# The order of a group's rows in device memory: channel by channel, or with the rows of channels eight apart next to each other

## The chip, the cores and the metric

The kernel runs on one core of a Trainium2 chip. Time is the device time of one execution in microseconds (us); it is 320.35 us as the median of 3 runs before the change (320.22 to 320.51).

## The reference, cut to what matters

```python
def _L0_cond_ref(x, subjects, weights):        # x: (128, 128, 1024), weights: (8, 128, 128), all f32
    w = weights[subjects]                      # one of 8 matrices for each of the 128 samples
    out = jnp.einsum('bct,bcd->bdt', x, w)
    return out
x = x + _L0_cond_ref(x, itok_B_0_7, L0_cond_weights)
```

Every sample is a matrix of 128 channels by 1024 times. It is multiplied by the weight matrix of its subject, and the sample itself is added. 64 MiB come in and 64 MiB go out.

## The kernel before, in words

The host lays x out by groups of GROUP = 4 samples: in a group each of the 128 channels has one row that holds its 4 samples of 1024 floats one behind the other, 16 KiB in all. A group is a block of 2 MiB, with the rows in the order of the channels (line 149). The output has the same layout and is turned back on the host (lines 157 and 158). There are 32 groups.

On the chip a ring of SLOTS = 8 slots in SBUF holds 8 groups, with the channels on the 128 partitions. The work of one group goes through these steps.

- SyncE (SP) issues the loads: first the weights (line 63), then the first 8 groups (line 65) with no wait, then the other 24 (lines 69 and 70), each once the store of the group that held the slot has landed.
- VectorE (DVE) adds the unit matrix to all 8 weight matrices once (line 111), so that one matmul gives product and residual together.
- GpSimd (POOL) reads the subject of each sample (line 84), waits at each group's first sample for its load (line 87) and copies the chosen matrix to one of 4 buffers (line 91).
- TensorE (PE) multiplies, two matmuls of 512 columns a sample (line 102), into one of 4 PSUM buffers of 1024 columns.
- DVE writes the products of even samples back into the slot (line 117), ScalarE (ACT) those of odd ones (line 128). The result takes the place of its own input.
- ACT issues the store of the group behind its last sample (line 133), after it has waited for both drains.

A load and a store each move one 2 MiB block. Loads go to the queue of SP (q1 in the profile), stores to that of ACT (q10); both are worked off by the same 16 DMA engines. `x_loaded[s]` and `stored[s]` are semaphores by slot; each takes 16 from every finished DMA. Line 137 is the end of the kernel: it waits for the last store of each slot.

Of the kernel before, what the change touches and what calls it, by code (L numbers as in the profile page):

```python
# [11 lines left out]
GROUP = 4  # L12

BUFS = 4
BANK = 512
DMA = 16


def subject_mix_kernel(nc: bass.Bass, x: bass.AP, subjects: bass.AP, weights: bass.AP, out: bass.AP):

    groups, channels, row = x.shape
    times = row // GROUP
    samples = groups * GROUP
    turns = groups // SLOTS
    per_turn = SLOTS * GROUP
    banks = times // BANK

    _, n_subjects, mixed = weights.shape
    assert channels == mixed == weights.shape[0] == 128 and banks * BANK == times and turns * SLOTS == groups
    assert GROUP == BUFS and 2 * BUFS == banks * BUFS  # L30

    with ExitStack() as ctx:
        def sem(name):
            return ctx.enter_context(nc.semaphore(name))


        ring = ctx.enter_context(nc.sbuf_tensor("ring", [channels, SLOTS, GROUP, times], F32))
        loaded = ctx.enter_context(nc.sbuf_tensor("loaded", [channels, n_subjects, mixed], F32))
        table = ctx.enter_context(nc.sbuf_tensor("table", [channels, n_subjects, mixed], F32))
        ones = ctx.enter_context(nc.sbuf_tensor("ones", [channels, mixed], F32))  # L40
        unit = ctx.enter_context(nc.sbuf_tensor("unit", [channels, mixed], F32))
        selected = ctx.enter_context(nc.sbuf_tensor("selected", [channels, BUFS, mixed], F32))
        subject_row = ctx.enter_context(nc.sbuf_tensor("subject_row", [1, samples], I32))
        products = ctx.enter_context(nc.psum_tensor("products", [mixed, BUFS, times], F32))

        subjects_loaded = sem("subjects_loaded")
        weights_loaded = sem("weights_loaded")
        ones_ready = sem("ones_ready")
        unit_ready = sem("unit_ready")
        table_ready = sem("table_ready")  # L50
        x_loaded = [sem(f"x_loaded{s}") for s in range(SLOTS)]
        stored = [sem(f"stored{s}") for s in range(SLOTS)]

        weights_selected = [sem(f"weights_selected{j}") for j in range(per_turn)]

        product_ready = sem("product_ready")
        even_drained = sem("even_drained")
        odd_drained = sem("odd_drained")

        with nc.Block() as block:  # L60
            @block.sync
            def _(sp):
                sp.dma_start(loaded[:], weights[:]).then_inc(weights_loaded, DMA)  # L63
                for s in range(SLOTS):
                    sp.dma_start(ring[:, s].rearrange("p j t -> p (j t)"), x[s]).then_inc(x_loaded[s], DMA)  # L65
                for group in range(SLOTS, groups):
                    turn, s = divmod(group, SLOTS)

                    sp.wait_ge(stored[s], turn * DMA)
                    sp.dma_start(ring[:, s].rearrange("p j t -> p (j t)"), x[group]).then_inc(x_loaded[s], DMA)  # L70

            @block.gpsimd
            def _(pool):
                nc.gpsimd.memset(ones[:], 1.0).then_inc(ones_ready, 1)  # L74
                pool.wait_ge(ones_ready, 1)

                nc.gpsimd.affine_select(unit[:], ones[:], [[-1, mixed]], ALU.is_equal, 0.0,  # L77
                                        base=0, channel_multiplier=1).then_inc(unit_ready, 1)
                pool.wait_ge(subjects_loaded, DMA)
                pool.wait_ge(table_ready, 1)  # L80
                for i in range(samples):
                    turn, j = divmod(i, per_turn)

                    subject = pool.value_load(subject_row[0:1, i:i + 1]).with_bounds(min_val=0, max_val=n_subjects - 1)  # L84
                    if j % GROUP == 0:

                        pool.wait_ge(x_loaded[j // GROUP], turn * DMA + DMA)
                    if i >= BUFS:

                        pool.wait_ge((even_drained, odd_drained)[i % 2], (i - BUFS) // 2 + 1)  # L90
                    nc.gpsimd.tensor_copy(selected[:, i % BUFS:i % BUFS + 1, :],  # L91
                                          table[:, bass.ds(subject, 1), :]).then_inc(weights_selected[j], 1)

            @block.tensor
            def _(pe):
                with pe.Fori(0, turns) as turn:
                    for j in range(per_turn):
                        s, g = divmod(j, GROUP)

                        pe.wait_ge(weights_selected[j], turn + 1)  # L100
                        for n in range(banks):
                            last = nc.tensor.matmul(products[:, j % BUFS, n * BANK:(n + 1) * BANK],  # L102
                                                    selected[:, j % BUFS, :],
                                                    ring[:, s, g, n * BANK:(n + 1) * BANK], start=True, stop=True)
                        last.then_inc(product_ready, 1)

            @block.vector
            def _(dve):
                dve.wait_ge(unit_ready, 1)
                dve.wait_ge(weights_loaded, DMA)  # L110
                nc.vector.tensor_tensor(table[:], loaded[:],  # L111
                                        unit[:].unsqueeze(1).to_broadcast([channels, n_subjects, mixed]),
                                        ALU.add).then_inc(table_ready, 1)
                for i in range(0, samples, 2):

                    dve.wait_ge(product_ready, i + 1)
                    nc.vector.tensor_copy(ring[:, i // GROUP % SLOTS, i % GROUP, :],  # L117
                                          products[:, i % BUFS, :]).then_inc(even_drained, 1)

            @block.scalar  # L120
            def _(act):
                act.dma_start(subject_row[:], subjects.rearrange("(a b) -> a b", a=1)).then_inc(subjects_loaded, DMA)
                for i in range(1, samples, 2):
                    group = i // GROUP
                    s = group % SLOTS

                    act.wait_ge(product_ready, i + 1)
                    nc.scalar.copy(ring[:, s, i % GROUP, :], products[:, i % BUFS, :]).then_inc(odd_drained, 1)  # L128
                    if i % GROUP == GROUP - 1:

                        act.wait_ge(even_drained, (i + 1) // 2)
                        act.wait_ge(odd_drained, (i + 1) // 2)  # L132
                        act.dma_start(out[group], ring[:, s].rearrange("p j t -> p (j t)")).then_inc(stored[s], DMA)


        for s in range(SLOTS):
            nc.scalar.wait_ge(stored[s], turns * DMA)
# [21 lines left out]
```

## Time and profile before

| | |
|---|---|
| median of 3 runs | 320.35 us (320.22 to 320.51) |
| the profiled execution | 320.11 us |
| its span, first to last instruction | 318.7 us |
| moved by DMA in the span | 134.80 MB, 423 GB/s on average |
| mean granted clock of TensorE | 0.942 |
| PE, DVE, ACT, POOL busy | 76%, 25%, 21%, 12% of the span |

The page of the profile gives shares of the span by engine, a row of 40 slices of the span (8 us each) with the share of time in which the DMA engines were busy and what they moved, the DMA queues with packets and bytes, the chain of waits that ended last, and groups of instructions. A packet is one row of 16 KiB for x and the output. Semaphore increments are packets of a few bytes of their own. A view by stretches gives the same for chosen parts of the span; its DMA share can read a little over 1, since a packet is counted whole in the stretch in which it starts. The view of DMA issues gives the time in which an issue holds its queue's engine, and the time from issue to landing.

### The profile page before, as it was taken

The page shows a single profiled execution, that of the slowest core. Times are in us where ns is not written, and L with a number is a line of the kernel's source. Part 1 is how long each engine was busy: PE and PEld are TensorE (multiplying, and loading weights), DVE is VectorE, ACT ScalarE, POOL GpSimd, SP SyncE. Part 2 cuts the span into 40 slices and gives each one's busy share as a digit, 9 for nine tenths or more (in the row PEclk, how much of TensorE's full clock was granted, in tenths as well). Part 3 has the DMA queues.
Part 4 walks back from the last instruction along what each step waited for, and adds up shares of the span by engine and source line. Part 5 has one row for each costly group of instructions (what it writes and reads, how often), then busy time and mean ns, then how long its engine had stood idle before and what let it go on. Part 6 is the DMA issues. An engine that isn't in the chain of part 4 may idle for free.

```text
span 318.7 us, 1718 instructions
## 1 busy us (share of the span) xinstructions
PE 242.5 (76%) x512; PEld 101.0 (32%) x512; DVE 79.6 (25%) x65; ACT 66.1 (21%) x65; POOL 38.6 (12%) x134
## 2 busy tenths in 40 slices
PE   0799999787868886669868668768698686787840
PEld 0344444233323332223333223323233232233310
DVE  1133433331313321223313133212233131331310
ACT  1033223211222212121212222112212122211220
POOL 0111111011110011100111101111001111011100
PEclk9999999997998999998979999979989799997995
DMA  8999999999999999999999999999999999999996
GB/s 300 430 424 393 428 429 426 432 434 436 436 428 430 428 428 430 431 432 437 436 428 430 428 428 430 432 431 434 431 434 430 430 428 430 430 434 434 430 436 290
DMA packets 9368, 134.80 MB, mean 423 GB/s; under 512 B 1041, under 2 KB 1042, under 8 KB 1170
## 3 DMA queue, kind: packets, MB, share of 16 engines
q1 hardware_dynamic: 4752, 67.64, 50.1%
q10 hardware_dynamic: 4610, 67.11, 49.2%
q14 instruction: 5, 0.04, 0.0%
q8 instruction: 1, 0.02, 0.0%
HBM read 67.63 MB, written 67.11 MB: 423 GB/s over the span
## 4 chain that ended last, share of the span: by engine, by line
DMA 81%; PE 10%; another core or an unknown queue 2%; ACT 1%; SPq 1%; POOLq 1%; issue 0%; DVE 0%; ACTq 0%
DMA ring<-x 51%; DMA out<-ring 30%; PE products L102 10%; ACT ring L128 1%; SPq L65 1%; POOLq L84 0%; DVE ring L117 0%; SPq L63 0%; POOLq L91 0%; ACTq L132 0%; POOLq L90 0%
## 5 line engine op out<-in xcount | busy, mean ns | idle before, releaser
L102 PE MATMUL products<-ring,selected 128*128 128x512 f32 x512 | 242.5, 631 | 63.6 <-POOL selected L91 63.6
L102 PEld LDWEIGHTS products<-ring,selected 128*128 128x128 f32 x512 | 101.0, 202 | 204.2 <-issue 119.1
L117 DVE COPY ring<-products 128x1024 f32<-128x1024 f32 x64 | 78.4, 1225 | 221.2 <-PE products L102 221.2
L128 ACT COPY ring<-products 128x1024 f32<-128x1024 f32 x64 | 64.8, 1012 | 239.7 <-PE products L102 239.7
L91 POOL COPY selected<-table 128x128 f32 x128 | 37.9, 296 | 261.7 <-DMA ring<-x 206.2
L111 DVE TENSOR_TENSOR table<-loaded,unit 128x1024 f32<-128x1024 f32 x1 | 1.2, 1226 | 4.7 <-DMA loaded<-weights 4.7
L128 ACT ACT_TABLE_LOAD x1 | 1.3, 1283 | 1.4 <-PEq L145 1.4
L77 POOL TENSOR_SCALAR_AFFINE_SELECT unit<-ones 128x128 f32<-128x128 f32 x1 | 0.3, 294 | 0.1
L74 POOL MEMSET ones<- 128x128 f32 x1 | 0.2, 205 | 0.3 <-POOLq L145 0.3
L145 POOL MEMSET const-float32-0.0<- 128x1 f32 x1 | 0.1, 99 | 0.3 <-issue 0.3
L145 POOL MEMSET const-bfloat16-1.0<- 128x1 bf16 x1 | 0.1, 102 | 0.0
L145 POOL MEMSET const-uint8-127<- 128x1 uint8 x1 | 0.1, 102 | 0.0
L145 POOL MEMSET const-float32-1.0<- 128x1 f32 x1 | 0.1, 99 | 0.0
## 6 DMA issues: line engine op xcount, KB each, us to landing
ring<-x SPq DMA_DIRECT2D x32, 2048.0 KB, 37.1
out<-ring ACTq DMA_DIRECT2D x32, 2048.0 KB, 30.8
loaded<-weights SPq DMA_DIRECT2D x1, 512.0 KB, 3.8
subject_row<-subjects ACTq DMA_DIRECT2D x1, 0.5 KB
```

Of the source, the lines that this page charges most:

```text
L65: sp.dma_start(ring[:, s].rearrange("p j t -> p (j t)"), x[s]).then_inc(x_loaded[s], DMA)
L74: nc.gpsimd.memset(ones[:], 1.0).then_inc(ones_ready, 1)
L77: nc.gpsimd.affine_select(unit[:], ones[:], [[-1, mixed]], ALU.is_equal, 0.0, base=0, channel_multiplier=1).then_inc(unit_ready, 1)
L91: nc.gpsimd.tensor_copy(selected[:, i % BUFS:i % BUFS + 1, :], table[:, bass.ds(subject, 1), :]).then_inc(weights_selected[j], 1)
L102: last = nc.tensor.matmul(products[:, j % BUFS, n * BANK:(n + 1) * BANK], selected[:, j % BUFS, :], ring[:, s, g, n * BANK:(n + 1) * BANK] ...
L111: nc.vector.tensor_tensor(table[:], loaded[:], unit[:].unsqueeze(1).to_broadcast([channels, n_subjects, mixed]), ALU.add).then_inc(table_r ...
L117: nc.vector.tensor_copy(ring[:, i // GROUP % SLOTS, i % GROUP, :], products[:, i % BUFS, :]).then_inc(even_drained, 1)
L128: nc.scalar.copy(ring[:, s, i % GROUP, :], products[:, i % BUFS, :]).then_inc(odd_drained, 1)
L145: nc = bacc.Bacc("TRN2", target_bir_lowering=False, num_devices=1)
```

## The change

The host splits the 128 channels as 16 parts of EACH = 8 (channel = 8 u + i, with u from 0 to 15 and i from 0 to 7) and writes the rows of a group in the order i, u: first channels 0, 8, 16, ... 120, then 1, 9, ... 121, and so on. In the block of 2 MiB the rows of channels 8 u + i and 8 (u + 1) + i are neighbours, 16 KiB apart; those of two channels in sequence are 16 rows (256 KiB) apart. The DRAM side of every load and store is an access pattern of three dimensions, 16 (u) by 8 (i) by 4096 floats, in the order of the channels; the SBUF side stays 128 partitions by 4096 floats. So each channel ends in the same partition as before, and nothing on the chip but the addresses of loads and stores differs.

```diff
+EACH = 8
...
-    groups, channels, row = x.shape
+    groups, each, parts, row = x.shape
+    channels = each * parts
...
+    x_rows = [x[group].rearrange("i u f -> u i f") for group in range(groups)]
+    out_rows = [out[group].rearrange("i u f -> u i f") for group in range(groups)]
...
-                    sp.dma_start(ring[:, s].rearrange("p j t -> p (j t)"), x[s]).then_inc(x_loaded[s], DMA)
+                    sp.dma_start(ring[:, s].rearrange("p j t -> p (j t)"), x_rows[s]).then_inc(x_loaded[s], DMA)
...
-                    sp.dma_start(ring[:, s].rearrange("p j t -> p (j t)"), x[group]).then_inc(x_loaded[s], DMA)
+                    sp.dma_start(ring[:, s].rearrange("p j t -> p (j t)"), x_rows[group]).then_inc(x_loaded[s], DMA)
...
-                        act.dma_start(out[group], ring[:, s].rearrange("p j t -> p (j t)")).then_inc(stored[s], DMA)
+                        act.dma_start(out_rows[group], ring[:, s].rearrange("p j t -> p (j t)")).then_inc(stored[s], DMA)
...
-    laid = x.reshape(groups, GROUP, channels, times).transpose(0, 2, 1, 3).reshape(groups, channels, GROUP * times)
+    parts = channels // EACH
+    laid = x.reshape(groups, GROUP, parts, EACH, times).transpose(0, 3, 2, 1, 4)
+    laid = laid.reshape(groups, EACH, parts, GROUP * times)
...
-    mixed = result.results[0]["out"].reshape(groups, channels, GROUP, times)
-    return np.ascontiguousarray(mixed.transpose(0, 2, 1, 3).reshape(samples, channels, times))
+    mixed = result.results[0]["out"].reshape(groups, EACH, parts, GROUP, times)
+    return np.ascontiguousarray(mixed.transpose(0, 3, 2, 1, 4).reshape(samples, channels, times))
```

## Rows read from the trace of the kernel before

**Rows 1.** The page: the chain of waits that ended last, shares by engine and line.
```profile
DMA 81%; PE 10%; another core or an unknown queue 2%; ACT 1%; SPq 1%; POOLq 1%; issue 0%; DVE 0%; ACTq 0%
DMA ring<-x 51%; DMA out<-ring 30%; PE products L102 10%; ACT ring L128 1%; SPq L65 1%; POOLq L84 0%; DVE ring L117 0%; SPq L63 0%; POOLq L91 0%; ACTq L132 0%; POOLq L90 0%
```

**Rows 2.** The page: the DMA lines of the 40 slices, and its queues.
```profile
DMA  8999999999999999999999999999999999999996
GB/s 300 430 424 393 428 429 426 432 434 436 436 428 430 428 428 430 431 432 437 436 428 430 428 428 430 432 431 434 431 434 430 430 428 430 430 434 434 430 436 290
...
q1 hardware_dynamic: 4752, 67.64, 50.1%
q10 hardware_dynamic: 4610, 67.11, 49.2%
```

**Rows 3.** The view of DMA queues, stretch 120:200: packets, MB, share of 16 engines.
```profile
q10 hardware_dynamic: 1182, 17.24, 50.3%
q1 hardware_dynamic: 1188, 17.22, 50.3%
```

**Rows 4.** By stretches: start:end us, length, PE, PEld, DVE, ACT, POOL, PEclk, DMA share, GB/s.
```profile
0.00:2.00 2.00, 0.00 (x0) 0.00 (x0) 0.00 (x0) 0.64 (x1) 0.70 (x6) 1.00 0.26 29
2.00:4.00 2.00, 0.00 (x0) 0.00 (x0) 0.00 (x0) 0.64 (x1) 0.00 (x0) 1.00 0.92 303
4.00:6.00 2.00, 0.00 (x0) 0.00 (x0) 1.23 (x1) 0.00 (x0) 0.00 (x0) 1.00 0.98 406
6.00:8.00 2.00, 0.00 (x0) 0.00 (x0) 0.00 (x0) 0.00 (x0) 0.00 (x0) 1.00 1.08 459
12.00:16.00 4.00, 4.00 (x7) 1.67 (x6) 1.23 (x1) 0.00 (x0) 0.30 (x1) 1.00 1.00 430
22.00:28.00 6.00, 6.00 (x16) 2.65 (x15) 2.16 (x2) 2.02 (x2) 0.89 (x3) 1.00 1.00 369
120.00:200.00 80.00, 60.24 (x129) 24.85 (x128) 19.60 (x16) 17.21 (x17) 9.48 (x32) 0.96 1.01 431
312.00:316.00 4.00, 0.00 (x0) 0.00 (x0) 0.00 (x0) 0.00 (x0) 0.00 (x0) 0.50 0.97 414
316.00:318.70 2.70, 0.00 (x0) 0.00 (x0) 0.00 (x0) 0.00 (x0) 0.00 (x0) 0.50 0.12 49
```

**Rows 5.** Who waited for whom, whole span: us in total, times, longest us.
```profile
POOL selected L91 <- DMA ring<-x: 206.2, 28, 8.3
PE products L102 <- POOL selected L91: 63.6, 27, 10.0
```

**Rows 6.** The same for SP's queue: us in total, times, longest us.
```profile
SPq L70 <- DMA out<-ring: 247.3, 24, 31.1
```

**Rows 7.** The issues by line: ns min/median/max, first and last start.
```profile
L65 SPq DMA_DIRECT2D ring<-x x8: 424/436/643, 1.2 to 4.8; - x8
L70 SPq DMA_DIRECT2D ring<-x x24: 327/328/328, 36.4 to 260.5; - x24
L133 ACTq DMA_DIRECT2D out<-ring x32: 338/338/376, 21.1 to 307.2; - x32
```

**Rows 8.** Landing: the page's issues (KB each, us), then stores alone (min/median/max).
```profile
ring<-x SPq DMA_DIRECT2D x32, 2048.0 KB, 37.1
loaded<-weights SPq DMA_DIRECT2D x1, 512.0 KB, 3.8
DMA to landing us min/median/max: 11.5/30.8/32.5
```

**Rows 9.** The DMA queues in 22:28, around the first store: packets, MB, share.
```profile
q1 hardware_dynamic: 119, 1.69, 80.0%
q10 hardware_dynamic: 32, 0.52, 20.4%
```

## Prediction

> **What bounds the kernel now.** I read the chain of waits first: 81% of the span is DMA, 51% loads and 30% stores, and only 10% TensorE [rows 1]. A chain can run through transfers that wait for their turn, so next come the slices: the 16 DMA engines are nine tenths busy or more in 38 of 40, and move 424 to 437 GB/s in all of these but one, with loads and stores at 50.1% and 49.2% of the engines' time [rows 2]. Those two are 99.3% of 318.7 us, or 316.5 us of work for each engine. The kernel is bound by DMA engine time, not by latency and not by an order of work.
>
> The waits agree: GpSimd stands 206.2 us for loads in total and TensorE only 63.6 us for GpSimd, while SP stands 247.3 us for stores before it may load again [rows 5, 6]. Compute has time to spare, and a slot is refilled as soon as its store has landed.
>
> How good is the engine time itself? In 120:200 the stores take 50.3% of 16 x 80 us for 17.24 MB. That is 643.8 us for 1052 rows of 16384 bytes: 612 ns a row, or 26.8 GB/s an engine. The loads give the same, 50.3% for 17.22 MB, 613 ns [rows 3]. Reading from device memory and writing to it cost the same to within 0.2%, in a mixed stream. Where only loads run (12:16, 430 GB/s) and where both do (120:200, 431) the rate is one and the same [rows 4]. If the order of rows in memory cost anything in the steady state, I would expect it to differ by direction or by mix. I read 612 ns as what one engine needs for 16 KiB, whatever lies at the memory's side.
>
> **The sum of the span.** 134.80 MB at 431 GB/s are 312.8 us. To these come the stretches that move less, each by length x (1 - rate / 431) [rows 4]: 0:2 at 29 GB/s 1.87 us, 2:4 at 303 0.59, 4:6 at 406 0.12, 6:8 at 459 -0.13, 22:28 at 369 0.86, 312:316 at 414 about 0.16, 316:318.7 at 49 2.39. Together 5.9 us, and 318.7 in all, the span. The profiled execution took 320.11 us, so 1.4 us lie outside of the span, and it is 0.24 us below the median of 320.35. My numbers are the span's changes added to the median.
>
> **The change part by part.**
>
> *The steady term, 312.8 us.* Bytes, rows (8192 of 16 KiB), queues and engines stay. Only addresses move. Below, the term has no room: no slice of 8 us is over 437 GB/s, and 437 in place of 431 would be 1.4%, 4.3 us, a bound that the chip would have to hold for all of the span where it touches it in five slices (four of 436, one of 437), which differ from the mean by three rows of 16 KiB in some 210, counted in one slice or the next [rows 2]. Above, the one row in which something at the memory's side goes slower is 22:28, 369 GB/s [rows 4]; if all ran so, the term would be 365 us. I take the value of the long stretch, 431, since both directions hold it: 0 us. The ends stay for the range.
>
> *The stall at 22:28, 0.86 us.* The first store is issued at 21.1 [rows 7]. In 22:28 the sixteen engines have 16 x 6 = 96 us. The loads hold 80.0% of it for 1.69 MB, which is 103 rows: 96 us x 0.800 / 103 = 746 ns a row, against 613 in the steady state. The stores beside them take 96 x 0.204 / 32 = 612 ns [rows 3, 9]. So 103 load rows are slowed by 133 ns on average when writing begins, 13.7 us over 16 engines, the same 0.86. This is the only place in the trace where rows are slow. It is tied to the first write to the output, which is still there after the change, so I leave it as it is; between nothing left (-0.86 us) and twice as long (+0.86 us).
>
> *Issue of the DMAs.* The pattern at the memory's side has one dimension more. The issues hold their engine 328 ns (loads), 338 (stores) and 436 (the first eight) [rows 7]. If an issue grew to the longest seen, 643 ns, it would be 0.3 us more on each of 24 loads and 32 stores. What hides it: a load is 37.1 us from issue to landing [rows 8], in which half of 431 GB/s moves 8.0 MB, so nearly four loads of 2.1 MB are in the queue at a time and the engines never run out; for the last store, 11.5 us to landing at 431 GB/s are 5.0 MB, of which 2.9 MB are stores ahead of it. Without that cover it would be 24 x 0.3 = 7 us, at most, for loads. At the start there is less cover: the first x rows come behind the weights, whose issue stays as it is and whose rows land 3.8 us after it [rows 8]. I take 0, and 0.2 us as the upper end for the first issue. A cheaper issue would gain nothing, by the same cover.
>
> *Compute and order.* POOL, PE, DVE and ACT get the same bytes in the same partitions. A load that lands 0.3 us later would be met by a GpSimd that waits 206.2 us for loads anyway [rows 5]: what is late is only the group's store, and a store joins a queue 30.8 us deep [rows 8]. Nothing new waits.
>
> Sum: 0 us. A change of 0.64 us (0.2%) is about what a measurement of this kernel can tell from none.
>
> **A rule that speaks against it.** The rows show that in the layout of before, where the rows of one group are one run of 2 MiB, each takes 612 ns and no more [rows 3]. The Trainium skill, "DMA: Bandwidth & Descriptors", Latency and other measured facts, has copies between memory tensors slow down as the pitch between partitions' rows becomes a large power of two: 207 GB/s a direction at 512 KiB where a full rate is 214, and 103 at 4 MiB. By an estimate from that page a 3.3% lower rate would put some 10 us on the time; after the change channels in sequence are 256 KiB apart and those eight apart 16 KiB, so the rule reads either way, and no trace here shows a pitch that slows.
>
> **The rivals.**
>
> *R1, the stall at the first store goes.* If it comes from sixteen writes (and sixteen reads) that open sixteen distant places, neighbours may pass it quicker. For it: it is the only place with slow rows. Against it: the loads alone began at distant places too and run at 430 in 12:16 [rows 4]. Gain at most 0.86 us, 319.5 us. 0.13.
>
> *R2, neighbouring rows collide.* Sixteen engines that start one step together would now read one stretch of 256 KiB instead of sixteen places 128 KiB apart; if the memory spreads its load by addresses coarser than a row, they would sit on fewer parts of it. Place: every load and store, in the first of the eight steps above all, since engines drift apart later. Price: if one step in eight runs at the 369 GB/s of 22:28 [rows 4], the steady term grows by 1/8 x (431/369 - 1) = 2.1%, 6.6 us, giving 326.9 us. It decides once the mean row is over 613.3 ns (612 + 0.2%). For it: the memory's side did slow rows once. Against: that a row needs no more than 612 ns leaves unknown how much room the memory has, and it is the weakest argument on both sides. 0.17.
>
> *R3, the sides are split differently.* The memory's side counts 16 x 8, the SBUF side 128. The generator of packets may hand the rows to engines in another way, and two engines may then go to the same part of SBUF at one time. The trace of before has no row for it. It would cost between nothing and a doubling of the steady term (two engines sharing what one has now); by the nearest row, 369 GB/s throughout, it is 365 - 313 = 52 us, 372 us. 0.10. The Trainium skill, "SBUF — State Buffer", Door 1: The DMA port swizzle, lets partitions p and p + 32 share a port, and "DMA: Bandwidth & Descriptors", The descriptor swizzle, gives each engine just the partitions of one port, in a transfer of 128 partitions; by those pages a split into eight partitions in sequence would make engines share ports, and no run here shows it.
>
> *R4, the change doesn't do what it says.* If an engine's eight rows are not eight channels in sequence, the sixteen rows of one step are not the sixteen neighbours. Then the addresses are only shuffled in the block, and the time stays at 320.3 us. By the Trainium skill, "DMA: Bandwidth & Descriptors", The descriptor swizzle (engine e of the first eight takes partitions 4e to 4e+3 and 32 more), neighbouring engines would start at channels 4 apart, 1 MiB apart in the new layout; no run here shows which rows an engine takes. 0.15, with the same number as my forecast.
>
> **How the numbers follow.** The forecast, that nothing is changed since the row time is the engines' own, has 0.45; with R4 that is 0.60 for within 0.2%. R1 gives 0.13 for faster; R2 and R3 0.27 for slower. Predicted: 320.3 us. Its own range is 319.8 to 320.9. The range of 8 in 10 takes in R1 (319.3, with 0.2 for the runs) and most of R2 (to 327.5), and leaves out R3 and the far part of R2, some 0.15.
>
> **What would show it.** Right: 612 ns a row in both queues in 120:200; 428 to 437 GB/s in the slices; the same 4752 and 4610 packets; the dip at 22:28 still there; issues of 330 to 650 ns and SP still waiting over 240 us. Wrong: a row time over 613.3 ns or a steady rate below 430 (R2; R3 if it is below 400 or the packets differ in number), a rate of 425 or more in 22:28 (R1), or idle DMA engines in the middle, which would mean that the issue had lost its cover. The step that I trust least is that 612 ns is the engine's own time and that the memory has room behind it.

## The result and the profile after

The changed kernel takes 374.83 us (median of 5 runs, 371.8 to 387.34), the kernel before 320.35 beside it (5 runs, 320.0 to 321.46): a ratio of 1.167, 95% interval 1.165 to 1.170. It was forecast at 320.3 with a range up to 327.5. The ratio leaves out the slowest execution, 387.34 us, which is the one profiled below (its granted clock is 0.879, that of the other four 0.878 to 0.892), so the sums that follow stand to 387 and not to 375.

The slices and the queues of the page, beside [rows 2]:

```profile
DMA  8999999999999999999999999999999999999968
GB/s 200 216 211 295 341 343 405 397 408 385 384 377 370 350 355 370 353 366 363 363 370 375 385 379 382 374 368 357 360 359 363 363 362 375 406 408 401 350 192 190
...
q1 hardware_dynamic: 4752, 67.64, 52.3%
q10 hardware_dynamic: 4610, 67.11, 46.5%
```

The same packets, the same bytes, engines as busy as before, and 5% to 56% less moved in a slice: each packet takes longer. The view by stretches of the changed kernel, beside [rows 4] (loads alone run in the first two), and its DMA queues in 120:200, beside [rows 3] (packets, MB, share of 16 engines):

```profile
4.00:20.00 16.00, 4.53 (x6) 2.04 (x7) 1.94 (x2) 0.00 (x0) 1.17 (x4) 1.00 1.02 218
12.00:16.00 4.00, 0.53 (x1) 0.50 (x2) 0.00 (x0) 0.00 (x0) 0.58 (x3) 1.00 1.04 221
22.00:28.00 6.00, 5.32 (x14) 2.10 (x13) 1.90 (x2) 1.26 (x2) 1.17 (x4) 1.00 1.02 216
120.00:200.00 80.00, 53.66 (x104) 21.90 (x103) 15.93 (x14) 13.16 (x13) 8.21 (x28) 0.88 1.01 363
```

```profile
q1 hardware_dynamic: 998, 14.52, 52.8%
q10 hardware_dynamic: 997, 14.52, 48.0%
```

In 120:200 the sixteen engines have 16 x 80 = 1280 us, and 14.52 MB are 886 rows: a load row takes 0.528 x 1280 / 886 us = 763 ns and a store row 0.480 x 1280 / 886 us = 693 ns, where both took 612 to 613. Where only loads run (12:16) the rate is 221 GB/s in place of 430. That is very nearly half, and a first hint of the cause: two engines doing the work of one. Against 431 GB/s, and by slices of 9.65 us, the first three slices lose 14.9 us, the last two 10.7 and the 35 between the rest of the 73.1 us by which the span is over 312.8: 47.5 us. Before, the whole loss was 5.9.

The issues of the changed kernel (lines 72 and 77 are the old 65 and 70), beside [rows 7], and who waited, beside [rows 5, 6]:

```profile
L72 SPq DMA_DIRECT2D ring<-x x8: 581/598/617, 1.2 to 5.7; - x8
L77 SPq DMA_DIRECT2D ring<-x x24: 536/537/537, 46.0 to 308.6; - x24
```

```profile
POOL selected L98 <- DMA ring<-x: 309.7, 32, 13.8
```

```profile
SPq L77 <- DMA out<-ring: 289.5, 24, 39.7
```

An issue holds SP 537 ns in place of 328. It delays nothing that shows, as SP waits 289.5 us for stores and the DMA engines are nine tenths busy or more from the second slice to the 38th. Compute waits more because loads come later; it is not the cause.

### The profile page after: what moved, and what is told of

Read it like the earlier page. It is cut to its first block, busy times and chain, and to the rows that moved or that the text cites. A ratio compares the mean times of both kernels' runs of the same rounds, so it can differ in the third digit from the quotient of the medians.

```text
span 385.9 us, 1718 instructions
## 1 busy us (share of the span) xinstructions
PE 266.6 (69%) x512; PEld 108.8 (28%) x512; DVE 79.6 (21%) x65; ACT 66.1 (17%) x65; POOL 38.2 (10%) x134
## 2 busy tenths in 40 slices
DMA packets 9368, 134.80 MB, mean 349 GB/s; under 512 B 1041, under 2 KB 1042, under 8 KB 1170
## 3 DMA queue, kind: packets, MB, share of 16 engines
q1 hardware_dynamic: 4752, 67.64, 52.3%
q10 hardware_dynamic: 4610, 67.11, 46.5%
## 4 chain that ended last, share of the span: by engine, by line
another core or an unknown queue 48%; PE 23%; DMA 11%; DVE 9%; POOLq 3%; issue 2%; SPq 1%; ACT 0%; POOL 0%
PE products L109 23%; DMA ring<-x 11%; DVE ring L124 9%; POOLq L91 2%; SPq L72 0%; POOLq L98 0%; ACT ring L135 0%; POOL selected L98 0%; POOLq L97 0%; SPq L70 0%
## 5 line engine op out<-in xcount | busy, mean ns | idle before, releaser
L109 PE MATMUL products<-ring,selected 128*128 128x512 f32 x512 | 266.6, 680 | 106.8 <-POOL selected L98 106.8
L109 PEld LDWEIGHTS products<-ring,selected 128*128 128x128 f32 x512 | 108.8, 218 | 263.7 <-POOL selected L98 132.5
```

## The experiments

Two accounts were set against each other, and within the first stands a question of its own. **S**, rival R3: the pattern of 16 x 8 makes each engine take the eight channels of one outer step, partitions 8u to 8u + 7, and two engines then use one way into SBUF. A way is meant as the part of the path to SBUF that certain partitions have in common; two engines whose partitions lie on one way are called partners, and they are in step when they use it at the same time. **M**, rival R2: rows that are neighbours in memory collide. The question is whether engines lose only while they are in step.

### The pattern without the new order, and the order without the pattern

The order of rows of before, with an unused row behind each eight, so that the pattern must stay 16 x 8 (against the changed kernel, cut; x and out are of groups, 16, 9, row):

```diff
-    x_rows = [x[group].rearrange("i u f -> u i f") for group in range(groups)]
-    out_rows = [out[group].rearrange("i u f -> u i f") for group in range(groups)]
+    x_rows = [x[group, :, 0:each, :] for group in range(groups)]
+    out_rows = [out[group, :, 0:each, :] for group in range(groups)]
...
```

> Theory S (split): the 16 x 8 pattern at the memory's side makes each engine take eight channels in sequence, and two engines then meet at one part of SBUF. Theory M (memory): neighbouring rows, 16 KiB apart, collide in device memory. This kernel has the order of rows of before, but with one unused row behind every eight, so that the pattern is 16 x 8 and can't be written as 128 rows. S expects the time of the changed kernel, 365 to 390 us, with loads alone (4:20) at about 218 GB/s and 1.2 us a row. M expects 320 to 322 us and 426 to 430 GB/s there.

Measured: 372.86 and 380.64 us, and 1.21 us a row with loads alone. By stretches, nearly the rates of the changed kernel (218, 216 and 363 GB/s):

```profile
4.00:20.00 16.00, 4.39 (x7) 1.91 (x8) 1.90 (x2) 0.00 (x0) 1.18 (x4) 1.00 1.02 219
22.00:28.00 6.00, 5.14 (x13) 2.03 (x12) 1.91 (x2) 1.07 (x2) 1.19 (x4) 1.00 1.00 218
120.00:200.00 80.00, 57.75 (x110) 23.59 (x110) 15.93 (x14) 14.17 (x14) 8.29 (x28) 0.87 1.01 367
```

The rows lie in the old order, and the loss is all there. So the new order in memory is not needed for it. The opposite test keeps the pattern of 128 rows and puts the rows 512 KiB apart (against the kernel before; the other loads and the stores alike):

```diff
-                    sp.dma_start(ring[:, s].rearrange("p j t -> p (j t)"), x[s]).then_inc(x_loaded[s], DMA)
+                    sp.dma_start(ring[:, s].rearrange("p j t -> p (j t)"), x[:, s]).then_inc(x_loaded[s], DMA)   # x: (channels, groups, row)
```

> The pattern of 128 rows of before, but each channel's rows of all groups lie one behind the other, so that the rows of one transfer are 512 KiB apart. S expects 320 to 322 us, since the split stays. M, in its general form (where a step's rows lie in memory sets the rate), expects a time clearly off 320: 325 to 335 us at this pitch, or more.

Measured: 320.6 us, ratio 1.0022 (1.0003 to 1.004), so at most 0.4% is lost, and in 120:200 the rate is the old one:

```profile
120.00:200.00 80.00, 63.15 (x131) 25.72 (x129) 20.35 (x17) 17.16 (x17) 9.39 (x32) 0.94 1.01 431
```

### Neighbours with another pattern: EACH = 4 and EACH = 2

```diff
-EACH = 8
+EACH = 4
```

> The changed kernel with EACH = 4: rows of channels four apart are neighbours, the pattern is 32 x 4. M expects 365 us or more, since the rows of channels in one step are neighbours as before or more so. S expects 365 to 390 us if engines still take eight channels in sequence, and about 320 us if a count of 32 lets the generator hand out blocks of four as it does with 128; either way it says nothing against S, but 320 us falls M.

Measured: 320.3 us, ratio 1.0008 (0.9996 to 1.002). Stretches, and the issues:

```profile
4.00:20.00 16.00, 10.22 (x21) 4.61 (x22) 3.68 (x3) 2.03 (x2) 2.37 (x8) 1.00 1.01 429
22.00:28.00 6.00, 6.00 (x15) 2.66 (x14) 2.25 (x2) 1.85 (x2) 0.89 (x3) 1.00 1.03 374
120.00:200.00 80.00, 61.57 (x131) 25.08 (x129) 20.31 (x17) 16.90 (x17) 9.48 (x32) 0.96 1.01 430
```

```profile
L77 SPq DMA_DIRECT2D ring<-x x24: 534/534/535, 35.1 to 260.7; - x24
```

Rows that are neighbours in memory are again those of a fixed distance in channels, and nothing is lost. M falls. So does any account by the third dimension of the pattern or the longer issue: this kernel has both, 534 ns an issue, at no cost. That part of the prediction's sum (0 us for the issue) is measured here by itself.

> The changed kernel with EACH = 2, a pattern of 64 x 2. With 32 x 4 the time was that of before. If the generator needs outer counts that make blocks of four channels or less, 64 x 2 is as good: 320 to 321 us. If it splits along the outer count into sixteen runs in sequence unless the count is one that it knows, 64 x 2 may fall back to eight channels in sequence: 365 to 390 us. S allows both; M (neighbouring rows in memory) is out already.

With EACH = 2 the time was 320.1 us, ratio 0.9997 (0.9986 to 1.0008). So 64 x 2, 32 x 4 and 128 rows are equal, and 16 x 8 stands alone.

### A direct test of the ways into SBUF

The order and the one-count pattern of before, but each transfer cut in two, of partitions 0 to 63 and 64 to 127 (the stores alike; the waits count two DMAs):

```diff
-                    sp.dma_start(ring[:, s].rearrange("p j t -> p (j t)"), x[s]).then_inc(x_loaded[s], DMA)
+                    sp.dma_start(ring[0:64, s].rearrange("p j t -> p (j t)"), x[s, 0:64]).then_inc(x_loaded[s], DMA)
+                    sp.dma_start(ring[64:128, s].rearrange("p j t -> p (j t)"), x[s, 64:128]).then_inc(x_loaded[s], DMA)
```

> The order of rows of before and patterns of one count (64 rows), but each load and store is cut into two DMAs, of channels 0 to 63 and 64 to 127. M expects 320 to 323 us. S in its port form (partitions 0 to 63 reach half of SBUF's ports) expects loads alone at about half the rate, 215 to 220 GB/s, and a time of 360 us or more; if the engines do not share by halves of the partitions, 320 to 323 us.

Measured: 388.13 and 400.95 us. The first stretch:

```profile
4.00:20.00 16.00, 4.52 (x6) 1.94 (x7) 1.93 (x2) 0.00 (x0) 1.17 (x4) 1.00 1.02 215
```

Half the rate again, with neither the new order in memory nor the 16 x 8 pattern. What the cut changes is the size of a transfer and which partitions the sixteen engines write at one time; to tell these two apart, the next kernel cuts at 32 and 96 instead, three DMAs a group:

```diff
+                    sp.dma_start(ring[32:96, s].rearrange("p j t -> p (j t)"), x[s, 32:96]).then_inc(x_loaded[s], DMA)
+                    sp.dma_start(ring[0:32, s].rearrange("p j t -> p (j t)"), x[s, 0:32]).then_inc(x_loaded[s], DMA)
+                    sp.dma_start(ring[96:128, s].rearrange("p j t -> p (j t)"), x[s, 96:128]).then_inc(x_loaded[s], DMA)
```

> The order of rows of before; each transfer is cut into three, of channels 32 to 95, 0 to 31 and 96 to 127. S with the map in which partitions 32 apart share a way into SBUF: the 64 of the first reach all the ways, four channels to an engine, at full rate; the 32 of each other reach half of them. Loads alone then average 431 / (1/2 + 1/2 x 2) = 287 GB/s, if the engines stay in step, more if the two small ones overlap; 215 to 220 would mean that any transfer under 128 partitions is slow, 425 to 430 that the cut at 64 was special. Time: 330 to 360 us by S.

Measured: 365.0 us (363.44 and 366.58), and for loads alone

```profile
4.00:20.00 16.00, 7.04 (x12) 3.16 (x13) 2.45 (x2) 1.01 (x1) 1.18 (x4) 1.00 1.01 275
```

275 GB/s against 287 worked out, and well over the 215 of the cut at 64, though the transfers are smaller and more. The time came out 5 us over the range given for it. Stretches of 1 us show the two rates by turns, here those in the middle of the start:

```profile
12.00:13.00 1.00, 0.04 (x1) 0.04 (x1) 0.00 (x0) 0.00 (x0) 0.29 (x1) 1.00 1.08 459
13.00:14.00 1.00, 1.00 (x2) 0.48 (x3) 0.00 (x0) 0.00 (x0) 0.65 (x3) 1.00 0.98 360
14.00:15.00 1.00, 1.00 (x3) 0.48 (x2) 0.00 (x0) 0.00 (x0) 0.24 (x1) 1.00 1.14 246
15.00:16.00 1.00, 1.00 (x3) 0.48 (x2) 0.00 (x0) 0.00 (x0) 0.00 (x0) 1.00 1.01 213
```

The packet records of the trace say the same: of the 269 load rows that start in 4:20, 98 take under 640 ns and 100 over 1150. In the changed kernel none of 213 takes under 1000 ns. So the 64 partitions of the middle are written at the full rate, and a transfer of 64 partitions is not slow for being small; 0 to 63 together, or 64 to 127 together, are slow. The Trainium skill, "SBUF — State Buffer", Door 1: The DMA port swizzle, has partitions 32 apart share one of sixteen ports, 0 to 63 reaching eight of them. These two runs agree with that map: 215 GB/s is half of the 429 before, and 275 is 4% under the 287.

### Loads alone, stores alone

Only x, or only the output, in the changed layout and pattern. The first, against the changed kernel (the second does the same to x_rows instead):

```diff
-    out_rows = [out[group].rearrange("i u f -> u i f") for group in range(groups)]
+    out_rows = [out[group] for group in range(groups)]
```

> Only the loads use the 16 x 8 pattern; the output keeps the order and the 128-row pattern of before. Theory S (engines that take eight channels in sequence meet at one part of SBUF): loads alone (4:20) at about 218 GB/s as in the changed kernel, the stores alone at the end at 425 to 438 GB/s, and a time between the two kernels, 335 to 360 us. Rival S2 (the slow part is the packets' own generation or decoding, whatever the direction): the same for the start, but in the mixed part the stores' rows keep 612 ns.

> Only the stores use the 16 x 8 pattern. S: loads alone (4:20) at 426 to 430 GB/s, stores alone at the end at about 190 to 230 GB/s as in the changed kernel, 335 to 360 us in all. If the loss were one of loads alone (writes into SBUF), the time would be 320 to 322 us.

Measured: 362.9 us with the loads (ratio 1.133, 1.128 to 1.138), 330.95 and 348.57 us with the stores. The queues in 120:200, first the kernel with changed loads:

```profile
q1 hardware_dynamic: 1096, 16.09, 52.7%
q10 hardware_dynamic: 1083, 15.79, 48.4%
```

and the one with changed stores:

```profile
q10 hardware_dynamic: 1172, 17.11, 51.2%
q1 hardware_dynamic: 1168, 16.97, 49.6%
```

With changed loads a load row takes 687 ns and a store row 643, though the stores are as before; they share their engines with slow loads, which may be why. Loads alone run at 216 GB/s there. With changed stores a store row takes 628 ns and a load row 613. In these executions, then, writing SBUF costs more than reading it; but the second is the one of 330.95 us, and its other execution took 348.57, so this is not shown in general. S2, by which the stores would keep 612 ns, does not hold. The two losses, 42.6 and 10.7 to 28.3 us, add up to 53 to 71 where both changes together cost 54.5. The time with loads is 3 us over the range given.

Both ends missed their numbers. With changed loads the stores alone at the end (345:360) come to 268 GB/s in place of 425 to 438, but because the engines work for 63% of the time; a row takes 619 ns, as S has it. With changed stores the last four slices read 372, 318, 366 and 181 GB/s, above the 190 to 230 given in three of four. Here are the stores alone near the end, first of the changed kernel in 370:384, then of this one in 316:326:

```profile
q10 hardware_dynamic: 173, 2.57, 76.9%
```

```profile
q10 hardware_dynamic: 226, 3.21, 78.2%
```

The first are 0.769 x 16 x 14 / 157 us = 1.10 us a row, the second 0.782 x 16 x 10 / 196 us = 0.64 us. The same stores with the same pattern, alone in both, are near to doubled in one kernel and near to the old 612 ns in the other. So the pattern by itself doesn't set the size of the loss. How the engines stand to each other may; these lines don't show it.

The slices of the kernel with changed loads show the same for loads:

```profile
GB/s 205 215 217 308 367 391 414 402 398 387 393 396 393 409 407 391 395 386 400 385 404 409 337 405 420 427 416 414 409 403 398 400 398 362 351 375 387 404 248 266
```

The transfers run at 217 GB/s in the third slice, where they are alone; mixed with stores they run at 427 in the 26th and at 337 three slices before that. It is no fixed tax.

### How many engines: EACH = 16

The changed kernel with EACH = 16 in the place of 8.

> EACH = 16, a pattern of 8 x 16. If the outer counts set the number of engines (the largest number up to 16 that divides both 8 and 128), only 8 engines work, each on 16 channels in sequence, and engines 0 and 2, 1 and 3 and so on share a way when in step: about 107 GB/s with loads alone (a quarter of 431), at most 215 in the mixed part, 620 to 1000 us in all. If 16 engines stay, the packet share is near 100% and the time 320 to 390 us.

Measured: 682.6 us, ratio 2.131 (2.112 to 2.151). Stretches of this kernel:

```profile
4.00:20.00 16.00, 0.00 (x0) 0.00 (x0) 1.22 (x1) 0.00 (x0) 0.00 (x0) 1.00 0.50 108
120.00:200.00 80.00, 36.04 (x64) 14.75 (x64) 9.80 (x8) 8.10 (x8) 4.70 (x16) 0.75 0.51 211
```

```profile
q1 hardware_dynamic: 547, 8.44, 25.4%
q10 hardware_dynamic: 547, 8.44, 25.1%
```

The DMA share is 0.50: half of the engines work. The Trainium skill, "DMA: Bandwidth & Descriptors", Why a DMA increments its semaphore by 16 and not by 1, has a DMA use as many engines as the largest number up to 16 that divides both outer counts, which is eight here; the trace agrees with its 0.50. With loads alone they reach 108 GB/s, half of what eight engines can, or 1.22 us a row (0.500 x 16 x 16 us for 105 rows). In 120:200 they reach 211, and a row takes 631 (loads) and 624 ns (stores). The channels of an engine and their order are the same in both stretches, and the loss of half seen at the start is all but gone in the mix.

The numbers suggest why, by an estimate that no run tests. If a way passes two rows every 1.22 us, as loads alone show, then in the mix two partners, which each write one row in 631 + 624 = 1255 ns, ask for no more than it passes. That would fit an engine that is slow at writing by itself as well; this run doesn't exclude one. Nor does it tell why sixteen engines lose 16% in the mix and these eight 1.5%.

### Seven tries to move partners out of step

If engines meet only while in step, a lead of half a transfer (4 of an engine's 8 rows) should cure the start. Small extra transfers ahead of the groups were to give such leads, on 12, 8 or 4 engines; first into a spare tensor, then from memory to memory. The first of them:

```diff
+                sp.dma_start(spare[0:48, 0, :], x_rows[0][0:12, 0:4, :]).then_inc(shifted, DMA)
+                sp.dma_start(spare[0:16, 1, :], x_rows[0][0:4, 0:4, :]).then_inc(shifted, DMA)
```

> The changed kernel with two small extra loads into a spare tensor ahead of the groups: 4 rows each on engines 0 to 11 (outer count 12) and 4 more on engines 0 to 3 (outer count 4), so that engines 0-3, 4-7, 8-11, 12-15 stand 8, 4, 4 and 0 rows back. S-step: an engine with eight channels in sequence takes four of them through one way into SBUF and four through the next, and engines e and e+4 are on the same way when in step; four rows apart they never meet. Expected: loads alone (4:20) well above 218, up to 431 GB/s, and 325 to 355 us in all. Rival S-fixed: an engine whose channels lie on two ways is slow by itself, whatever its partner does: 218 GB/s and 370 us or more, plus 2.4 us for the extra rows.

> As the run before but 8 rows in place of 4 in each extra load: the partners stand 8 rows apart, a whole transfer, and so are in step again. S-step: loads alone at about 218 GB/s, 370 to 385 us. If a shift of any size helps (because it is only disorder that helps), the rate is as high as with 4 rows.

> Only engines 0 to 7 are put 4 rows back (one extra load with an outer count of 8). If partners are e and e+4, both stay in step: 218 GB/s in 4:20 and 368 to 385 us. If partners are e and e+8 (of two halves), all pairs are apart: up to 431 GB/s.

> Only engines 0 to 3 are put 4 rows back. Partners e and e+4: the pairs of the first eight engines are apart, those of the other eight in step, so loads alone run at (431 + 218) / 2 = 325 GB/s at the start, and the whole lies between the run with all pairs apart and the changed kernel, 345 to 372 us. S-fixed: 218 GB/s.

> As the first shifted kernel (4 rows on engines 0 to 11, 4 on 0 to 3), but the extra rows go to partitions 32 to 79 and 64 to 79 of the spare tensor. In the first one the extra loads themselves met: engines 8 to 11 wrote partitions 32 to 47, beside engines 0 to 3 on 0 to 15, so that the two groups came out of them by other than 4 rows. Counting each row at 611 ns, and at twice that where two engines are on one way (way = bits 2 to 4 and bit 6 of the partition), gives 260 GB/s for loads alone in 14:30 of the first and 390 to 396 here. S-step: 350 to 396 GB/s in 14:22. S-fixed, or a wrong map of the ways: no better than the first (266 to 299).

> The changed kernel with the same two extra transfers (4 rows on engines 0 to 11, 4 on 0 to 3), but from memory to memory, so that they touch no part of SBUF and can't meet there. S-step: engines e and e+4 then stand just 4 rows apart when the groups begin, and loads alone run at 400 to 431 GB/s in 14:22. If the way into SBUF pulls partners into step whatever their start, or if partners are others than e and e+4, the rate is 210 to 290 as in the runs with the spare tensor.

> The same with 8 rows in each extra transfer: partners stand a whole transfer apart and are in step. S-step: 210 to 225 GB/s in 22:30, where the extra rows are through, and 375 to 390 us in all. If a shift of any size helps, the rate is as high as with 4 rows.

| kernel | us (2 runs) | 4:20, GB/s | 14:22, GB/s | expected, GB/s |
|---|---|---|---|---|
| the change | 371.8 to 387.34 (5 runs) | 218 | 209 | |
| 4 rows, spare | 365.91, 372.34 | 222 | 276 | up to 431 (4:20) |
| 8 rows, spare | 383.14, 389.08 | 216 | 219 | 218 (4:20) |
| 4 rows on engines 0 to 7 | 374.87, 381.2 | 225 | 213 | 218 (4:20) |
| 4 rows on engines 0 to 3 | 365.79, 371.14 | 225 | 242 | 325 (the start) |
| 4 rows, other partitions | 370.43, 387.3 | 197 | 223 | 350 to 396 (14:22) |
| 4 rows, memory to memory | 376.1, 381.64 | 250 | 229 | 400 to 431 (14:22) |
| 8 rows, memory to memory | 370.19, 374.13 | 331 | 221 (22:30) | 210 to 225 (22:30) |

The extra rows still run in 4:20, and those from memory to memory raise the rate there, so 14:22 is the fairer stretch; but the first kernels were forecast for 4:20, and by that stretch the first gave 222, no better than the change. The two with 8 rows, and the one that was to leave partners together, gave about the rates expected (the times are up to 5 us off their ranges). Of the four with partners apart none reached its number, and the first also missed its range of 325 to 355 us by 11 us and more. 276 is the best, and the one whose extra rows touch no part of SBUF, from memory to memory, gave 229, and 233 in 22:30, where the one with 8 rows gave 221. The rows by stretches of two of them, into the spare tensor and from memory to memory, both with 4 rows:

```profile
14.00:22.00 8.00, 0.00 (x0) 0.00 (x0) 0.00 (x0) 0.00 (x0) 0.00 (x0) 1.00 0.99 276
```

```profile
14.00:22.00 8.00, 2.77 (x4) 1.22 (x5) 0.00 (x0) 0.00 (x0) 1.17 (x4) 1.00 0.98 229
```

The 276 GB/s speak against S-fixed, an engine that is slow by itself: it could not pass 218, whatever extra rows ran before. That being in step is what costs, and which engines are partners, is not shown. Either the transfers of 12 and of 4 outer steps don't run on the engines that I took for them, or the partners are others, or they are drawn back into step. These runs don't tell which, and the way in which two engines meet stays open.

## Why the prediction was wrong

**The step that failed** is the first of the sum: "The steady term ... Bytes, rows (8192 of 16 KiB), queues and engines stay. Only addresses move." Bytes, rows, queues and the number of engines did stay (4752 and 4610 packets). What did not stay, by the rates above, is which partitions each engine serves: the change altered the outer count of the memory's side from 128 to 16. The term was put at 312.8 us and unchanged; the profiled execution moves the same 134.80 MB at 349 GB/s on average, 386 us, with load rows of 1.23 us where loads run alone and of 763 ns in the mix. The row time of 612 ns [rows 3] was read as the engine's own, "whatever lies at the memory's side". As a statement on the memory it held: rows 512 KiB apart or neighbours cost 0.4% at most (320.6 and 320.3 us). It left out the other side of the transfer, SBUF, where the trace of before shows no loss (429 GB/s in 4:20).

**R3 was the mechanism**, as far as it is shown, and had 0.10. Its sign, a steady rate below 400 GB/s, is what came. Its price, 372 us from 369 GB/s throughout, lies 3 us from the median, by luck: the 369 was the rate beside the first store, another matter, and the profile has 363 GB/s in the middle and 190 to 216 at the two ends. "Between nothing and a doubling" was right; the doubling is what loads alone show. The range left R3 out, and that was the second error: the change put two different outer counts, 16 and 128, on the two sides of each DMA, a form that no row of before vouched for, and a case that can cost 50 us deserved more than one in ten.

**R2** was wrong in mechanism (neighbours at EACH = 4 cost nothing). **R1**: the dip at the first store is still there with neighbours, 374 GB/s in 22:28 at EACH = 4, so the order of rows does not cause it. **R4** put its weight on engines not taking eight channels in sequence. The equal rates of the change and of its pattern in the old order (218 and 219 GB/s for loads alone) fit engines that do take them. The engine of a packet is in no record, so this is inferred from rates.

**The smaller steps** held. The issue grew by 0.21 us (328 to 537 ns), within the 0.3 allowed, and cost nothing (EACH = 4). The rule on the pitch of rows decided nothing. The Trainium skill, "DMA: Bandwidth & Descriptors", Latency and other measured facts, has it for copies between memory tensors, 207 GB/s for 214 at 512 KiB; between memory and SBUF the rate at that pitch is 431 GB/s here, without that loss. Compute only waited more.

The idea behind the change, neighbours in one step, is worth nothing here even where it costs nothing: EACH = 4 and 2 are within 0.2% of before. No version beat it, and with engines 99% busy at 612 ns a row and a loss of 5.9 us in the whole span there is little left to win in the order of rows.

## What to carry to other kernels

Keep the outermost count of both sides of a DMA at the 128 partitions, or at a count tested to be as good (on the memory's side 64 and 32 were; 16 cost 17% and 8 doubled the time). Don't cut a transfer at partition 64: that alone took the kernel from 320 to 388 us and more. Before changing a layout that adds a dimension to a transfer's pattern, ask which partitions each DMA engine will touch, not only where the rows lie in memory. Full DMA engines are no proof that they do full work: look at bytes per busy time, here 612 ns against 763 for the same row, and at a stretch in which only one direction runs, where the cause stands undiluted (430 against 218 GB/s).

## What the runs showed of the hardware that was not expected

- Where the engines share ways, by the account above, the rate with loads alone is half (215 to 219 GB/s in four kernels), but in a mix with stores only 1% to 16% goes (426 to 363 GB/s in 120:200), and with eight engines almost nothing (211 GB/s, of at most 214 by 612 ns a row).
- Run to run the slowed kernels scatter far more than the sound ones: 371.8 to 387.34 us for the change, 330.95 to 348.57 with changed stores, against 319.5 to 321.46 for the kernel before in all its runs. Why is open.
- In the mix, writes into SBUF suffer more than reads from it in the executions profiled (687 against 628 ns a row). Alone, reads can suffer as much: 1.10 us a row in 370:384 of the changed kernel. The 190 GB/s of its last slice is that, and engines that stand idle: the DMA share of the last two slices is six and eight tenths.
